# Key and value projections dealt anew around the third attention and the last attention's opening, and one key rotation moved behind two sums in the routed part

## The chip, the core and the metric

The kernel runs on one core of a Trainium2 chip. The core has five engines that each work through their own list of instructions and meet at semaphores: PE (TensorE: matrix products and transposes, written to eight PSUM banks), DVE (VectorE) and ACT (ScalarE), which both read PSUM, POOL (GpSimd), which works on SBUF, and SP (SyncE), which issues the DMAs here. The metric is the time of one execution on the device, in microseconds (us).

## What is computed

Eight layers work on x, 8 batches of 128 tokens of 512 numbers. Each takes the layer norm of x and adds its result to x:

```python
x = x + _L1_ffn_ref(_layernorm(x, axis=-1), ...)
x = x + _L2_xattn_ref(_layernorm(x, axis=-1), ctx_4096, L2_xattn_conv_w, L2_xattn_bn_gamma, L2_xattn_bn_beta)
x = x + _L2_ffn_ref(_layernorm(x, axis=-1), L2_ffn_W_base, L2_ffn_b_base, L2_ffn_W_router, L2_ffn_lora_A, L2_ffn_lora_B)
x = x + _L3_xattn_ref(_layernorm(x, axis=-1), ctx_4096, ctx_4096, mask_BxSxS2_ff0, L3_xattn_wq, L3_xattn_wk, L3_xattn_wv, L3_xattn_wo, 0)
x = x + _L3_ffn_ref(_layernorm(x, axis=-1), L3_ffn_route_w, L3_ffn_A, L3_ffn_Bw)
```

The change lies in three of them.

The third attention (`_L2_xattn_ref`) is not an attention by scores. It splits the channels into two sets, takes the maximum and the mean of each set for every token channel, runs a convolution of 7 taps over them, normalises the result over the whole batch, and scales the two sets with the sigmoids that come out.

The routed part (`_L2_ffn_ref`) is `x @ W_base.T + b_base` plus low-rank products of the two best of 8 experts.

The last attention (`_L3_xattn_ref`) has 32 query heads and 8 key and value heads of width 128. Queries and keys are turned by position: `x * cos + _rotate_half(x) * sin`. Its keys and values come from `ctx_4096`, an input, and not from x.

## The kernel before

**Work ahead.** Since the last attention's keys and values depend on the inputs alone, the kernel makes them earlier, in places where PE has time. The class `KeysAhead` (line 1632) deals them in 48 units: units 0 to 15 are halves of a key head (128 x 512 in PSUM), units 16 to 47 are values of one batch for two heads (128 x 256). One unit is 12 matmuls on PE: four chunks of the depth, each as hi x hi, hi x lo, lo x hi (lines 36 to 38). The units take turns in PSUM banks 6 and 7. Four methods hand the next units on, in the order in which the code calls them:

- `multiply(pe, count)`: PE makes the next `count` units. Unit u waits until unit u - 2 has been drained (`wait(pe, self.drained, u - 1)`, line 1698).
- `drain(act, count)`: ACT copies them from PSUM to `kv_keys` (line 1718) or `kv_values` (line 1721).
- `high(act, i)` and `low(pool, i)`: ACT and POOL split item i of the weights in two parts (lines 1685 and 1689). `high` of item i waits until all units of item i - 2 are made.
- `rotate(dve, count)` and `join(pool, count)`: DVE turns the next halves of the keys, each with two products into `kv_cross` (lines 1759 and 1760) and one into `kv_keys` (line 1764). POOL adds the two (line 1745).

**Third attention** (`l2_attention`, line 2121). It begins with `norm_stage` (line 109): DVE scales x to `l2x_xn` (line 136), PE turns it (line 171), ACT and DVE copy the turned batches out (lines 192 and 149). Its `pe_first` lets PE make three units ahead of the transposes. A block ends with a barrier of all engines. In the next block DVE masks four chunks (`l2x_fc`, line 2277), POOL takes the difference (`l2x_xn`, line 2182), DVE takes maxima and sums, and ACT takes the other means (line 2238, eight small instructions for each of six chunks). PE makes seven units meanwhile, and then turns the statistics (`l2x_stat`, line 2205). From there on it is a chain: the convolution on DVE (from line 2292), a product on PE, the mean and variance of the batch with two small products on PE (line 35, `l2x_zmv` and `l2x_dev`), the tanh on ACT (line 2253), transposes of the map on PE (line 2219), the scaling on ACT and DVE, transposes back (line 2227) and the sums to x (line 2344). PE makes three units beside the convolution, two behind the map and four behind the transposes back.

**Routed part** (`routed_ffn`, line 2349). PE makes 7 units and the first three base products, turns the weighted low-rank outputs (line 2445), and finishes batch after batch. Three PSUM banks serve the outputs: `base_product(b)` waits until DVE has added batch b - 3 to x (`wait(pe, o_read, b - 2)`, line 2430). DVE, which has its own list, rotates four halves of the keys before its first sum (line 2532), and one more before each of the sums 3 to 7.

**Last attention** (`l3_layer`, line 2658). `norm_stage` again, with three units ahead of the transposes and a split of the turned x in hi (ACT, line 184) and lo (DVE, line 141). In the next block PE projects the first query head in two halves, makes five units, and starts the scores of head 0 when POOL has joined both halves of the query. DVE rotates the two halves of the query (lines 1759, 1760, 1764 with `l3x_cross` and `l3x_q`), then two halves of the keys, and then masks the scores (line 3057). Eight groups of four heads follow; the first one still rotates three halves of the keys, and ACT copies the values (`l3x_v`, line 3015) when all sixteen are joined.

## Time and profile before

| | |
|---|---|
| Time, median of 3 runs | 1884.34 us (1883.32 to 1886.83) |
| Time of the profiled execution | 1882.91 us |
| Its span, first to last instruction | 1881.1 us |
| PE busy | 96% of the span |
| DVE, ACT, POOL busy | 72%, 34%, 33% |
| Mean granted clock of TensorE | 0.991 |
| DMA, mean | 42 GB/s |

The span is 1.8 us shorter than the time of its own execution. A row of the timeline gives the start and the length of one or more instructions in us from the span's start, then the engine, the line, what is written and read, and in brackets how long the engine sat idle before it, and what ended that. TensorE's granted clock is 1.00 at full speed (2.4 GHz) and 0.50 at half (1.2 GHz).

### The profile page before, as it was taken

What the parts mean: (1) busy time and instruction counts of PE and PEld (TensorE: products, weight loads), DVE (VectorE), ACT (ScalarE), POOL (GpSimd) and SP (SyncE); (2) the same over time, 40 slices, a digit from 0 to 9 for tenths busy, and PEclk for the clock granted to TensorE, in tenths of its full rate; (3) what the DMA queues carried; (4) which work ended last, traced back from release to release, by engine and by line L of the source; (5) the groups of instructions that cost most, each with busy time, mean ns of one, the idle gap of its engine ahead of it and who ended that gap; (6) DMA issues with size and microseconds to landing.
All of it is one profiled execution on the core that took longest, in us unless ns stands there. A gap on an engine that the chain in (4) does not pass through costs nothing. (4 is left out here: it accounts for less than half of the span.)

```text
span 1881.1 us, 29023 instructions
## 1 busy us (share of the span) xinstructions
PE 1802.9 (96%) x10418; PEld 1524.4 (81%) x10418; DVE 1348.7 (72%) x2778; ACT 636.4 (34%) x1749; POOL 615.0 (33%) x366
## 2 busy tenths in 40 slices
PE   7999999999999999998998998879899999999998
PEld 6888888899988888896876665665788888888886
DVE  5666676666666666657537877779788888888886
ACT  4312222222222221224025765530343343343333
POOL 6423322232223323323241003425433333334331
PEclk9999999999999999999999998989999999999999
DMA  4101111111001111110010002010101111110011
GB/s 172 59 7 50 50 52 49 52 49 52 25 23 52 49 52 49 52 54 23 23 45 20 1 26 68 23 63 1 45 24 45 34 33 33 34 33 33 34 34 46
DMA packets 29879, 78.44 MB, mean 42 GB/s; under 512 B 3856, under 2 KB 10704, under 8 KB 29424
## 3 DMA queue, kind: packets, MB, share of 16 engines
q1 hardware_dynamic: 29808, 77.50, 12.3%
q8 instruction: 44, 0.72, 0.2%
q14 instruction: 27, 0.22, 0.0%
HBM read 75.39 MB, written 2.10 MB: 41 GB/s over the span
## 5 line engine op out<-in xcount | busy, mean ns | idle before, releaser
L637 POOL TENSOR_TENSOR l0x_comb<-l0x_neg,l0x_bias 128x1024 f32<-128x1024 f32 x32 | 76.5, 2390 | 428.1 <-DVE l0x_probs L1002 305.2
L900 ACT ACTIVATE l0x_probs_t<-bank 128x512 f32<-128x512 f32 x32 | 19.1, 597 | 539.2 <-PE bank L753 539.2
L2795 POOL TENSOR_TENSOR l3x_q<-l3x_q,l3x_cross 128x512 f32<-128x512 f32 x64 | 89.7, 1406 | 194.4 <-DVE l3x_q L1764 194.4
L38 PE MATMUL bank<-l0x_w_v_hi,ctx_lo 128*128 128x256 f32 x512 | 144.9, 283 | 0.0
L37 PE MATMUL bank<-l0x_w_v_lo,ctx_hi 128*128 128x256 f32 x512 | 144.9, 283 | 0.0
L36 PE MATMUL bank<-l0x_w_v_hi,ctx_hi 128*128 128x256 f32 x512 | 144.9, 283 | 0.0
L886 ACT ACTIVATE l0x_probs<-l0x_probs,l0x_top 128x129 f32<-128x129 f32 x256 | 99.4, 390 | 61.1 <-DVE l0x_top L1006 61.1
L2981 ACT ACTIVATE l3x_probs<-l3x_probs,l3x_top 128x128 f32<-128x128 f32 x256 | 99.1, 388 | 38.1 <-DVE l3x_top L3062 38.0
L629 POOL TENSOR_TENSOR l0x_w_qk_lo<-l0x_raw_qk,l0x_w_qk_hi 128x1024 fp32r<-128x1024 f32 x31 | 75.0, 2420 | 110.5 <-ACT l0x_w_qk_hi L893 110.5
L36 PE MATMUL bank<-l3x_qin_hi,l3x_w_q_hi 128*128 128x512 f32 x256 | 105.8, 413 | 5.4 <-PEq L121 3.1
L36 PE MATMUL bank<-ctx_hi,l0x_w_qk_hi 128*128 128x512 f32 x256 | 100.8, 394 | 8.4 <-DVE ctx_lo L1113 8.4
L36 PE MATMUL bank<-l0x_qin_hi,l0x_w_qk_hi 128*128 128x512 f32 x256 | 105.4, 412 | 3.0 <-DVE l0x_qin_lo L1137 1.6
L1038 DVE TENSOR_TENSOR x<-x,bank 128x512 f32<-128x512 f32 x120 | 82.1, 684 | 33.2 <-PE bank L38 33.2
L37 PE MATMUL bank<-l3x_qin_lo,l3x_w_q_hi 128*128 128x512 f32 x256 | 100.7, 393 | 0.0
L38 PE MATMUL bank<-ctx_hi,l0x_w_qk_lo 128*128 128x512 f32 x256 | 100.6, 393 | 0.0
L37 PE MATMUL bank<-ctx_lo,l0x_w_qk_hi 128*128 128x512 f32 x256 | 100.5, 393 | 0.0
L38 PE MATMUL bank<-l3x_qin_hi,l3x_w_q_lo 128*128 128x512 f32 x256 | 100.5, 393 | 0.0
L38 PE MATMUL bank<-l0x_qin_hi,l0x_w_qk_lo 128*128 128x512 f32 x256 | 100.0, 391 | 0.0
L37 PE MATMUL bank<-l0x_qin_lo,l0x_w_qk_hi 128*128 128x512 f32 x256 | 99.9, 390 | 0.0
L37 PEld LDWEIGHTS bank<-l0x_w_v_lo,ctx_hi 128*128 128x128 f32 x512 | 98.2, 192 | 0.6
L36 PEld LDWEIGHTS bank<-l0x_w_v_hi,ctx_hi 128*128 128x128 f32 x512 | 98.2, 192 | 0.6
L38 PEld LDWEIGHTS bank<-l0x_w_v_hi,ctx_lo 128*128 128x128 f32 x512 | 98.2, 192 | 0.0
(474 smaller groups left out, 5222.2 us busy)
## 6 DMA issues: line engine op xcount, KB each, us to landing
l0x_raw_qk<-L_qk_dram SPq DMA_DIRECT2D x31, 512.0 KB, 4.7
l0x_raw_v<-L_v_dram SPq DMA_DIRECT2D x16, 512.0 KB, 5.6
l0x_raw_o<-L_o_dram SPq DMA_DIRECT2D x16, 512.0 KB, 5.3
l3x_raw<-L_q_dram SPq DMA_DIRECT2D x16, 512.0 KB, 3.4
l3x_raw<-L_o_dram SPq DMA_DIRECT2D x16, 512.0 KB, 3.4
kv_raw<-L_kv_dram SPq DMA_DIRECT2D x8, 512.0 KB, 3.5
l0x_ctx_raw<-ctx_t_dram SPq DMA_DIRECT2D x4, 512.0 KB, 5.9
x<-x_dram SPq DMA_DIRECT2D x8, 256.0 KB, 8.0
```

Of the source, the lines that this page charges most:

```text
L36: pe.matmul(out, lhs[0], rhs[0], start=start, stop=False)
L37: pe.matmul(out, lhs[0], rhs[1], start=False, stop=False)
L38: return pe.matmul(out, lhs[1], rhs[0], start=False, stop=stop)
L629: pool.tensor_tensor(f(w[1]), f(raw), as_f32(f(w[0])), ALU.subtract).then_inc(ready, 1)
L637: pool.tensor_tensor(comb[:, :, :], neg[:, :, :], bias[:, j:j + 1, :].to_broadcast([P, B, P]), ALU.add).then_inc(comb_ready, 1)
L886: act.activation(probs[j][:, b, :], probs[j][:, b, :], ACT.Exp, bias=top[:, b:b + 1], accum_out=row_sum[:, b:b + 1]).then_inc(exp_done, 1)
L900: act.activation(probs_t[:, 0:BH, :], bank[6][:, :].rearrange("p (b n) -> p b n", b=BH), ACT.Copy).then_inc(t_act, 1)
L1038: dve.tensor_tensor(x[:, b, :], x[:, b, :], bank[b % 4][:, :], ALU.add).then_inc(ring_drained, 1)
L2795: pool.tensor_tensor(dst[:, part], dst[:, part], cross[n][:, :], ALU.add).then_inc(rotated, 1)
L2981: act.activation(probs[j % 2][:, b, :], probs[j % 2][:, b, :], ACT.Exp, bias=top[:, b:b + 1], accum_out=row_sum[:, b:b + 1]).then_inc(exp_ ...
```

## The change

Nothing is computed that was not computed before, and no instruction is added or removed. Units, drains, rotations and joins change their places:

```diff
         def keys_before(act):
-            ahead.drain(act, 2)
+            ahead.drain(act, 1)
             ahead.high(act, 6)
             ahead.drain(act, 1)
 
-        norm_stage(core, xn, xt, loads, banks=6, pe_first=lambda pe: ahead.multiply(pe, 3), act_first=keys_before,
-                   pool_then=lambda pool: ahead.low(pool, 6))
+        norm_stage(core, xn, xt, loads, banks=6, pe_first=lambda pe: ahead.multiply(pe, 2), act_first=keys_before,
+                   pool_then=lambda pool: ahead.low(pool, 6), pe_then=lambda pe: ahead.multiply(pe, 1))
...
-                ahead.multiply(pe, 7)
+                ahead.multiply(pe, 6)
                 pe.wait_ge(stat_done, 1)
...
                 product(pe, bank[3][0:SETS * B, 0:1], [group], [dev[:, :]], True, True).then_inc(var_full, 1)
+                ahead.multiply(pe, 1)
                 pe.wait_ge(map_in, 1)
...
                         last.then_inc(means_done, 1)
-                        if (k, c) == (0, 1):
-                            ahead.drain(act, 2)
-                        if (k, c) == (0, 2):
-                            ahead.drain(act, 1)
+                        ahead.drain(act, 1)
+                        if (k, c) == (0, 3):
                             ahead.high(act, 7)
-                        if (k, c) == (1, 0):
-                            ahead.drain(act, 2)
                 ahead.drain(act, 2)
                 ahead.high(act, 8)
-                ahead.drain(act, 3)
+                ahead.drain(act, 2)
                 act.wait_ge(tanh_in, 1)
                 act.activation(z[:, :], z[:, :], ACT.Tanh, scale=0.5).then_inc(tanh_out, 1)
+                ahead.drain(act, 1)
                 act.wait_ge(map_done, 1)
...
                 if ahead:
-                    ahead.rotate(dve, 4)
+                    ahead.rotate(dve, 3)
                 if base:
                     dve.wait_ge(biased, B)
                 for b in range(B):
-                    if ahead and b >= 3:
+                    if ahead and b >= 2:
                         ahead.rotate(dve, 1)
...
             norm_stage(core, xn, qin, first_loads, first_high, first_low, banks=6,
-                       pe_first=lambda pe: ahead.multiply(pe, 3))
+                       pe_first=lambda pe: ahead.multiply(pe, 3), pe_then=lambda pe: ahead.multiply(pe, 2))
...
+                ahead.join(pool, 1)
                 rotate_both(0, q[0])
-                ahead.join(pool, 2)
+                ahead.join(pool, 1)
...
                 project_both(0, 0, w_q[0], 0, qin)
-                ahead.multiply(pe, 5)
+                ahead.multiply(pe, 3)
...
+                ahead.rotate(dve, 1)
                 for n in range(2):
                     rotate(n, 0, 0, 0, q[0], 0)
-                ahead.rotate(dve, 2)
+                ahead.rotate(dve, 1)
```

In the third attention the norm's PE work is now two units, the transposes, one unit (unit 4). The six units 5 to 10 stand ahead of the statistics' transposes, and unit 14 stands between the product of the variance and the transposes of the map. ACT drains one unit behind each of its six means. This is ACT's list behind the norm's copies, before and after; `l2x_stat` are the means, `kv_keys` the drains, `kv_w_hi` the weights' hi part. Before:

```order
L2238 ACTIVATE bank,l2x_stat<-l2x_fc 128x128 x16
L1718 ACTIVATE kv_keys<-bank 128x512 x2
L2238 ACTIVATE bank,l2x_stat<-l2x_fc 128x128 x8
L1718 ACTIVATE kv_keys<-bank 128x512
L1685 ACTIVATE kv_w_hi<-kv_raw 128x1024
L2238 ACTIVATE bank,l2x_stat<-l2x_fc 128x128 x8
L2238 ACTIVATE bank,l2x_stat<-l2x_xn 128x128 x8
L1718 ACTIVATE kv_keys<-bank 128x512 x2
```

And after:

```order
L2239 ACTIVATE bank,l2x_stat<-l2x_fc 128x128 x8
L1718 ACTIVATE kv_keys<-bank 128x512
L2239 ACTIVATE bank,l2x_stat<-l2x_fc 128x128 x8
L1718 ACTIVATE kv_keys<-bank 128x512
L2239 ACTIVATE bank,l2x_stat<-l2x_fc 128x128 x8
L1718 ACTIVATE kv_keys<-bank 128x512
L2239 ACTIVATE bank,l2x_stat<-l2x_fc 128x128 x8
L1718 ACTIVATE kv_keys<-bank 128x512
L1685 ACTIVATE kv_w_hi<-kv_raw 128x1024
L2239 ACTIVATE bank,l2x_stat<-l2x_xn 128x128 x8
L1718 ACTIVATE kv_keys<-bank 128x512
```

The first drain moved from behind the second mean to behind the first, and the weights' hi part from behind the third to behind the fourth.

In the routed part DVE's list changes around the first sums (`x<-x,bank` is a sum, the three lines ahead of it a rotation). Before, from the last of the four rotations on:

```order
L1759 TENSOR_TENSOR kv_cross<-kv_keys,kv_rope 64x512
L1760 TENSOR_TENSOR kv_cross<-kv_keys,kv_rope 64x512
L1764 TENSOR_TENSOR kv_keys<-kv_keys,kv_rope 128x512
L2532 TENSOR_TENSOR x<-x,bank 128x512
L88 BN_STATS stats<-x 128x6
L2532 TENSOR_TENSOR x<-x,bank 128x512
L88 BN_STATS stats<-x 128x6
L2532 TENSOR_TENSOR x<-x,bank 128x512
L88 BN_STATS stats<-x 128x6
```

And after, from the first sum on, which now follows the third rotation:

```order
L2530 TENSOR_TENSOR x<-x,bank 128x512
L88 BN_STATS stats<-x 128x6
L2530 TENSOR_TENSOR x<-x,bank 128x512
L88 BN_STATS stats<-x 128x6
L1759 TENSOR_TENSOR kv_cross<-kv_keys,kv_rope 64x512
L1760 TENSOR_TENSOR kv_cross<-kv_keys,kv_rope 64x512
L1764 TENSOR_TENSOR kv_keys<-kv_keys,kv_rope 128x512
L2530 TENSOR_TENSOR x<-x,bank 128x512
```

One rotation moved from ahead of the first sum to ahead of the third.

In the last attention two value units moved from behind the first query head to behind the norm's transposes, and DVE's list at the head of the block changes. Before:

```order
L1759 TENSOR_TENSOR l3x_cross<-bank,kv_rope 64x512
L1760 TENSOR_TENSOR l3x_cross<-bank,kv_rope 64x512
L1764 TENSOR_TENSOR l3x_q<-bank,kv_rope 128x512
L1759 TENSOR_TENSOR l3x_cross<-bank,kv_rope 64x512
L1760 TENSOR_TENSOR l3x_cross<-bank,kv_rope 64x512
L1764 TENSOR_TENSOR l3x_q<-bank,kv_rope 128x512
L1759 TENSOR_TENSOR kv_cross<-kv_keys,kv_rope 64x512
```

And after:

```order
L1759 TENSOR_TENSOR kv_cross<-kv_keys,kv_rope 64x512
L1760 TENSOR_TENSOR kv_cross<-kv_keys,kv_rope 64x512
L1764 TENSOR_TENSOR kv_keys<-kv_keys,kv_rope 128x512
L1759 TENSOR_TENSOR l3x_cross<-bank,kv_rope 64x512
L1760 TENSOR_TENSOR l3x_cross<-bank,kv_rope 64x512
L1764 TENSOR_TENSOR l3x_q<-bank,kv_rope 128x512
```

One rotation of the keys moved ahead of the two of the query; POOL's join of it moved in the same way.

## Rows read from the trace of the kernel before

**Rows 1.** Busy time and granted clock by stretch: us, PE, PEld, DVE, ACT, POOL, clock, DMA.

```profile
1224.00:1228.00 4.00, 0.56 (x5) 0.26 (x4) 2.27 (x8) 0.00 (x0) 0.33 (x1) 0.70 0.01 2
1228.00:1231.00 3.00, 0.04 (x1) 0.05 (x1) 1.90 (x4) 0.63 (x1) 0.20 (x1) 0.50 0.00 0
...
1338.00:1340.00 2.00, 1.92 (x5) 1.57 (x6) 0.00 (x0) 0.00 (x0) 0.00 (x0) 0.56 0.54 123
...
1390.00:1830.00 440.00, 439.72 (x2504) 382.91 (x2503) 374.60 (x513) 170.14 (x574) 152.08 (x86) 1.00 0.10 34
```

**Rows 2.** Timeline of DVE in the third attention.

```profile
1191.75 9.02 DVE L2277 TENSOR_TENSOR l2x_fc<-l2x_xt,crucial 128x1024 f32<-128x1024 f32 x4 [0.62 <-PEq L121]
...
1212.07 0.17 DVE L2286 TENSOR_SCALAR l2x_stat<-l2x_stat 128x16 f32<-128x16 f32 x1
1215.00 0.68 DVE L2292 COPY l2x_padded<-bank 32x512 f32<-32x512 f32 x1 [2.75 <-PE bank L2205]
```

**Rows 3.** Timeline of PE in the third attention.

```profile
1186.75 3.65 PE L171 MATMUL bank<-ident,l2x_xn 128*128 128x128 f32 x32
...
1208.71 0.47 PE L36 MATMUL bank<-kv_ctx_hi,kv_w_hi 128*128 128x512 f32 x1 [1.65 <-POOL kv_w_lo L1689]
...
1214.26 0.60 PE L2205 MATMUL bank<-ident,l2x_stat 128*32 128x128 f32 x4
...
1223.14 1.03 PE L35 MATMUL bank<-l2x_acc,l2x_pick 32*16 32x512 f32 x2
...
...
1230.95 0.61 PE L2219 MATMUL bank<-ident,l2x_z 16*128 16x16 f32 x4 [3.55 <-DVE l2x_z L2327]
1231.49 0.80 PE L36 MATMUL bank<-kv_ctx_hi,kv_w_hi 128*128 128x512 f32 x1
...
1236.35 0.28 PE L36 MATMUL bank<-kv_w_hi,kv_ctx_hi 128*128 128x256 f32 x1
```

**Rows 4.** Timeline of ACT in the third attention.

```profile
1207.99 1.05 ACT L1718 ACTIVATE kv_keys<-bank 128x512 f32<-128x512 f32 x2
```

**Rows 5.** Timeline of DVE in the routed part.

```profile
1294.81 0.69 DVE L1759 TENSOR_TENSOR kv_cross<-kv_keys,kv_rope 64x512 f32<-64x512 f32 x1
1295.50 1.66 DVE L1760 TENSOR_TENSOR kv_cross<-kv_keys,kv_rope 64x512 f32<-64x512 f32 x1
...
1297.81 0.68 DVE L2532 TENSOR_TENSOR x<-x,bank 128x512 f32<-128x512 f32 x1
...
1311.78 0.69 DVE L2532 TENSOR_TENSOR x<-x,bank 128x512 f32<-128x512 f32 x1 [0.73 <-PE bank L35]
```

**Rows 6.** Timeline of PE in the routed part.

```profile
1293.23 2.84 PE L35 MATMUL bank<-l2f_w_b,l2f_ht 128*128 128x512 f32 x6 [0.25 <-ACT l2f_ht L2471]
1298.63 1.10 PE L35 MATMUL bank<-l2f_w_base,l2f_xt 128*128 128x512 f32 x2 [2.56 <-DVE x L2532]
...
1303.00 3.60 PE L35 MATMUL bank<-l2f_w_base,l2f_xt 128*128 128x512 f32 x8
```

**Rows 7.** Timeline of PE at the last attention's opening.

```profile
1333.72 1.22 PE L171 MATMUL bank<-ident,l3x_xn 128*128 128x128 f32 x8 [1.05 <-DVE l3x_qin_lo L141]
1338.08 0.63 PE L36 MATMUL bank<-l3x_qin_hi,l3x_w_q_hi 128*128 128x512 f32 x1 [3.13 <-PEq L121]
...
1345.22 0.28 PE L36 MATMUL bank<-kv_w_hi,kv_ctx_hi 128*128 128x256 f32 x1
...
1352.41 1.95 PE L35 MATMUL bank<-kv_keys,l3x_q 128*128 128x128 f32 x16
...
1374.01 0.50 PE L36 MATMUL bank<-l3x_qin_hi,l3x_w_q_hi 128*128 128x512 f32 x1 [2.24 <-ACT l3x_v L3015]
```

**Rows 8.** Timeline of DVE at the last attention's opening.

```profile
1345.42 0.69 DVE L1759 TENSOR_TENSOR l3x_cross<-bank,kv_rope 64x512 f32<-64x512 f32 x1 [0.64 <-PE bank L38]
...
1347.55 0.69 DVE L1759 TENSOR_TENSOR kv_cross<-kv_keys,kv_rope 64x512 f32<-64x512 f32 x1
...
1353.74 1.36 DVE L3057 SCALAR_TENSOR_TENSOR l3x_probs<-bank,last_mask 128x512 f32<-128x512 f32 x2
```

## Prediction

> **What bounds the kernel now.** I read the windows first. Through the last attention's groups PE is busy for 439.72 of 440 us at full clock [rows 1]. So that stretch is PE's, and a head start or a delay that it gets at its opening comes out at the end of the kernel unchanged. Then I read PE's list for the places where it stands still between two layers, and asked for each who is late. There are four that the change touches.
>
> In the third attention the statistics' transposes start at 1214.26 [rows 3], though DVE finished the statistics at 1212.07 + 0.17 = 1212.24 [rows 2], and DVE then waits 2.75 us for them [rows 2]. Here PE is late: seven units stand ahead of the transposes. Behind the product of the variance it is PE that waits, 3.55 us [rows 3]. In the routed part PE waits 2.56 us for DVE's first sum [rows 6]. At the last attention's opening PE waits 3.13 us for the block's barrier, and then works at a granted clock of 0.56 [rows 7, 1].
>
> **Third attention, up to the statistics.** One 128 x 512 unit costs PE 2.78 us: two of them lie between 1208.71 and 1214.26, 5.55 us with the fill [rows 3]. Two units instead of three ahead of the norm's transposes let these begin at 1186.75 - 2.75 = 1184.0 [rows 3]. ACT has its drain and one weight split to do first, but copies the last batches in time, since it is paced by PE there. The transposes issue for 3.5 us, unit 4 follows for 2.75 us and the tail of its last matmul, so PE ends at about 1190.4. Before, the barrier followed 0.62 us behind DVE's last copy [rows 2]. The same 0.62 behind PE gives 1191.05 for DVE's start instead of 1191.75 [rows 2], so 0.7 us is gained and not 2.75, since PE is now the last at the barrier. If unit 4 hid nothing at all, the term would be 0; if the barrier needed nothing behind PE, 1.3.
>
> From its start to the finished statistics DVE needs 1212.24 - 1191.75 = 20.5 us [rows 2], so these are done at 1211.5. PE must have finished six units by then. Its bound is ACT: unit u waits for the drain of unit u - 2. The 1.65 us ahead of 1208.71 are laid to POOL's weight split by the view, but unit 10 needs unit 8 drained, and that is the first half of ACT's pair at 1207.99 [rows 3, 4]. Dealt one by one, ACT reaches the drain of unit 8 at about 1206.7 (0.7 earlier as the block is, and one drain less in its way), so unit 10 runs from 1207.3 to 1210.2. That is 1.3 us ahead of the statistics. If ACT were 1.3 us later than I count, the gain would shrink with it. The transposes start at about 1211.6 instead of 1214.26: **2.65 us**. Behind them PE has three units as before, and 1214.26 to 1223.14 [rows 3] is 8.9 us both for PE and for DVE's convolution; both shift alike.
>
> **Unit 14 in the gap.** It starts 0.1 us behind the variance product. PE stood idle for 3.55 us between that product and the transposes of the map [rows 3]. At full clock it takes 2.8 us and is hidden. But PE has done next to nothing since the convolution's product: the granted clock is 0.70 over 1224 to 1228, and 0.50 behind that [rows 1]. Its successor at half clock took from 1231.49 to 1236.35, 4.9 us and a tail of 0.15 [rows 3]; in the gap that is 1.5 to 1.6 us too long, and ACT, DVE and POOL all wait for the map. The bounds are 0 and 1.6. The stretch of the 0.70 row is the very place, so I take the middle, **0.8 us lost**. What it frees behind the map is worth nothing: there PE makes two units either way, while ACT scales.
>
> The Trainium skill ("TensorE: Matmul & The Clock Gate", Part 1) says that the array falls to 1.2 GHz when idle, and that the counting runs free, so that the point varies from run to run. The rows show the fall, not yet the spread. By this rule unit 14 would cost something between nothing and 1.6 us, another amount in each run, and the sum below would scatter by as much.
>
> **Routed part.** The fourth rotation starts at 1294.81 and the first sum at 1297.81 [rows 5]: it is 3.0 us long, as one of its products took 1.66 us and not 0.69 [rows 5], with POOL's join beside it. With three rotations the first sum starts at 1294.8 and is done at 1295.5. Its product is ready: three outputs are made from 1293.23 to 1296.07 [rows 6], one each 0.95. So base product 3 is free at 1295.5 and PE takes it when it is through with the third output, at 1295.9, instead of 1298.63 [rows 6]: **2.7 us**. From there on PE is the slower of the two; DVE waited 0.73 us for each of the later sums [rows 5]. The moved rotation costs DVE 2.1 to 3.1 us ahead of the third sum, which then comes at 1299.5 to 1300.5. Base product 5 needs it. A batch of PE's is 1303.00 - 1298.63 = 4.4 us long [rows 6], so that is two batches behind 1295.9, at 1304.6. That is 4 us of cover. If it were gone, every us more would come off the 2.7. POOL's join of that rotation moves with it and is waited for by nobody before the next rotation but one. The stage ends with PE's three units and their drain, so the whole 2.7 goes on.
>
> **Last attention's opening.** From PE's start to the scores pass 1352.41 - 1338.08 = 14.33 us [rows 7]. Of these, the five units are 7.19 us [rows 7], 1.44 each; two of them go to the norm, 2.88 us. The projection of the first head, 24 matmuls, takes 1345.22 - 1338.08 = 7.14 us [rows 7], where the same number took 5.55 at full clock [rows 3]. PE had stood still for 3.13 us. With two units in that gap, from 1334.8 to 1337.8, it should not fall, and 1.6 us come back. Against that stand 0.2 us, since PE's tail is now as late at the barrier as DVE. Sum: **4.3 us**; if the clock falls all the same, 2.7.
>
> DVE must follow. Before, it rotated the second half of the query from 1345.42 to 1347.55, two halves of keys from there to 1353.74, 3.1 each, and took the scores at 1353.74, 1.33 behind their start [rows 8, 7]. Now one rotation fits ahead of the query: it starts with the block, takes 2.1 us, and the query's first half comes out of PE 2.9 us in. The second half is out at 1343.9, rotated at 1346.0, the one key behind it at 1349.1. PE's scores start at 1348.1, and DVE wants them at 1349.4. POOL's join of the second query half, 1.8 us at most, ends at 1347.9, so PE, DVE and POOL meet within 0.3 us. Moving only the units or only the rotation would give little. Behind the scores nothing changes: three rotations stay in the first group, and PE's wait of 2.24 us for the values' copy [rows 7] stays with them.
>
> **The sum.** 2.65 - 0.8 + 2.7 + 4.3 = 8.85 us. Against the profiled execution that is 1882.91 - 8.9 = 1874.0. The median of the runs was 1884.34, 1.4 us above that execution, so I forecast 1884.34 - 8.9 = **1875.4 us**.
>
> **The rivals.**
>
> *The clock takes part of it.* Unit 14 runs wholly at 1.2 GHz (0.8 us more) and the opening's projection too (1.6 us). For: both stand next to idle stretches, and rows 1 show half clock at both places. Against: at the opening the idle time is filled. 8.9 - 2.4 = 6.5 us gained, 1877.8 us. Chance 0.17.
>
> *The head start of the last attention is given back.* The first group waits for the joined keys and for ACT's copy of the values. If that chain, or the DMA of the mask that is issued with the block, did not move with the scores, the 4.3 us would end in a longer wait than 2.24 there. Against: the chain is counted from the scores on, in the same order. 4.6 us gained, 1879.7 us. Chance 0.10. With the clock's losses too, 1882.1 us, no difference to speak of: 0.05.
>
> *Slower: a long stretch at half clock.* In the last attention PE has no idle time, so every us at 1.2 GHz there costs 0.5 us. The new timing would have to drop the clock after PE's 2.24 us wait and hold it for long: from 17.8 us of half clock on the 8.9 are eaten, from 25.4 us on the kernel is more than 0.2% slower, with 1888.2 us or more. The row of 440 us at 1.00 [rows 1] speaks against it. Chance 0.03.
>
> **How the numbers follow.** The forecast has 0.65; its own range is 1872.8 to 1877, from unit 14 free and 0.6 more at the barrier, and a median lower by the 1.4 us that lie between profile and median here, up to unit 14 at 1.6 and an opening 0.8 short. Adding the first rival and the nearer part of the second gives 1872.8 to 1879.2. A measurement of this kernel tells 0.2%, 3.8 us, from no change: below 1880.6 lie the forecast and the first two rivals, 0.92; 0.05 lies within; 0.03 above.
>
> **What would show it.** In the profile after: the statistics' transposes within 0.3 us of DVE's last statistic, and DVE's 2.75 us wait below 1; unit 14 either 2.8 us long, or up to 5 us with matmuls of 0.8 us and a map that waits for it; no wait of PE for DVE's sum in the routed part; no half clock at the last attention's opening, and 10 us from PE's start there to the scores. The prediction is wrong if PE, and not DVE, is again the last at the statistics, or if PE's wait for the values' copy grows from 2.24 to 5 us or more.

## The result, and the profile after

| | before | after |
|---|---|---|
| Time, median of 6 runs each | 1884.2 us (1883.32 to 1887.37) | 1876.67 us (1875.39 to 1878.11) |
| Time of the profiled execution | 1882.91 us | 1875.39 us |
| Its span | 1881.1 us | 1873.6 us |
| Mean granted clock | 0.991 | 0.991 |

The ratio of the times is 0.995, with a 95% interval of 0.9938 to 0.9961. The interval lies below 1, so the kernel is faster, by 7.5 us or 0.4%. PE is busy for nearly the same time, 1805.0 us after and 1802.9 before, 96% of the span in both.

I compare stages by the time that has passed since the third attention's norm began (DVE's first L131 there; at 1178.35 before, 1177.88 after). What lies ahead of that point is untouched, and the point moved by up to 5 us between the profiles of this study, so its own place says nothing about the change.

| us from the norm's start | before | after | earlier |
|---|---|---|---|
| DVE's statistics done | 33.89 | 33.17 | 0.72 |
| their transposes on PE | 35.91 | 33.24 | 2.67 |
| transposes of the map on PE | 52.60 | 50.95 | 1.65 |
| transposes back on PE | 64.39 | 62.55 | 1.84 |
| next norm begins | 76.48 | 75.26 | 1.22 |
| last attention's norm begins | 147.01 | 142.98 | 4.03 |
| scores of head 0 on PE | 174.06 | 165.78 | 8.28 |
| first `l3x_heads_lo` on DVE | 203.84 | 196.88 | 6.96 |
| end | 702.75 | 695.72 | 7.03 |

The last row and the 0.47 us of the starting point make the 7.5; the 0.47 are no work of the change. PE's timeline in the third attention, after; start, length and work in us, and in brackets the idle time ahead and what ended it:

```profile
1211.12 0.61 PE L2205 MATMUL bank<-ident,l2x_stat 128*32 128x128 f32 x4 [0.96 <-DVE l2x_stat L2284]
...
1224.16 0.20 PE L35 MATMUL bank<-l2x_dev,l2x_mean 16*16 16x1 f32 x2 [1.07 <-DVE l2x_dev L2315]
1224.29 0.50 PE L36 MATMUL bank<-kv_ctx_hi,kv_w_hi 128*128 128x512 f32 x1
...
1228.83 0.42 PE L2220 MATMUL bank<-ident,l2x_z 16*128 16x16 f32 x4
...
1240.43 6.24 PE L2228 MATMUL bank<-ident,l2x_fc 128*128 128x128 f32 x32 [6.81 <-DVE l2x_fc L2338]
```

PE now waits for the statistics and not they for PE (against the row at 1214.26 in [rows 3]). Unit 14 fills the gap, but it takes all from 1224.29 to 1228.83, and the map's transposes wait for nothing but it. The transposes back, 6.24 us here, come behind 6.81 us of idle. DVE's timeline there:

```profile
1190.57 9.01 DVE L2275 TENSOR_TENSOR l2x_fc<-l2x_xt,crucial 128x1024 f32<-128x1024 f32 x4 [2.62 <-PEq L121]
...
1210.88 0.17 DVE L2284 TENSOR_SCALAR l2x_stat<-l2x_stat 128x16 f32<-128x16 f32 x1
1211.87 0.68 DVE L2290 COPY l2x_padded<-bank 32x512 f32<-32x512 f32 x1 [0.81 <-PE bank L2205]
...
1253.14 0.64 DVE L131 BATCH_NORM_AGGREGATE mv<-stats 128x2 f32<-128x6 f32 x8 [0.93 <-PEq L2166]
```

DVE waits 0.81 us for the statistics' transposes where it waited 2.75 [rows 2], but 0.93 us at the barrier that ends the layer. The granted clock by stretch (us, PE, PEld, DVE, ACT, POOL, clock, DMA): unit 14, the transposes back, and the first group of the last attention behind PE's wait for the values' copy:

```profile
1224.00:1226.00 2.00, 1.83 (x8) 1.49 (x9) 1.03 (x4) 0.00 (x0) 0.53 (x1) 0.79 0.01 4
1226.00:1228.00 2.00, 2.00 (x7) 1.52 (x6) 1.13 (x3) 0.63 (x1) 0.00 (x0) 0.50 0.00 0
...
1240.00:1246.00 6.00, 5.57 (x28) 5.57 (x29) 4.69 (x8) 0.71 (x2) 2.35 (x1) 0.53 0.00 0
...
1334.00:1344.00 10.00, 10.00 (x63) 9.01 (x63) 8.39 (x11) 1.35 (x5) 4.37 (x3) 1.00 0.33 107
...
1365.00:1367.00 2.00, 2.00 (x5) 1.62 (x6) 1.97 (x3) 1.91 (x5) 1.05 (x1) 0.53 0.00 0
1367.00:1369.00 2.00, 2.00 (x7) 1.52 (x7) 1.94 (x4) 2.00 (x11) 1.33 (x1) 0.62 0.00 0
```

The row of 1334 to 1344 is the last attention's opening, all of it at full clock, where 0.56 was granted over two of these microseconds [rows 1]. The last two rows are new. This is the same place in the kernel before, right behind the same wait, at a clock of 1.00:

```profile
1374.00:1376.00 2.00, 1.99 (x9) 1.65 (x10) 1.97 (x3) 1.91 (x5) 1.02 (x1) 1.00 0.00 0
```

The timeline of PE shows the routed part and the opening, after:

```profile
1292.49 1.88 PE L35 MATMUL bank<-l2f_w_b,l2f_ht 128*128 128x512 f32 x4
1294.21 3.60 PE L35 MATMUL bank<-l2f_w_base,l2f_xt 128*128 128x512 f32 x8
...
1333.79 0.47 PE L36 MATMUL bank<-l3x_qin_hi,l3x_w_q_hi 128*128 128x512 f32 x1 [0.32 <-PEq L121]
1343.66 0.80 PE L35 MATMUL bank<-kv_keys,l3x_q 128*128 128x128 f32 x5
...
1364.98 0.69 PE L36 MATMUL bank<-l3x_qin_hi,l3x_w_q_hi 128*128 128x512 f32 x1 [1.89 <-ACT l3x_v L3014]
```

The fourth base product, the first of the row at 1294.21, follows without a wait (2.56 us in [rows 6]). The barrier costs PE 0.32 us instead of 3.13 and the scores start 9.87 us behind the projection instead of 14.33 [rows 7]. The wait for the values' copy is 1.89 us (2.24 before).

**Where the time went.** Ahead of the scores 8.28 us are gained. The first group gives 1.3 back. The loss lies between the start of ACT's copy of the values and the first `l3x_heads_lo`, a stretch of 10.9 us that was 9.3 before.

### The profile page after: what moved, and what is told of

It is laid out like the page before. It is cut to its first block and busy times, and to the rows that moved or that the text cites. A ratio compares the mean times of both kernels' runs of the same rounds, so it can differ in the third digit from the quotient of the medians.

```text
span 1873.6 us, 29023 instructions
## 1 busy us (share of the span) xinstructions
PE 1805.0 (96%) x10418; PEld 1525.9 (81%) x10418; DVE 1345.4 (72%) x2778; ACT 635.6 (34%) x1749; POOL 614.0 (33%) x366
```

## The experiments: each part alone

The three parts of the change were put one by one into the kernel before. The diffs are against it.

**The third attention's part alone**

```diff
-            ahead.drain(act, 2)
+            ahead.drain(act, 1)
...
-        norm_stage(core, xn, xt, loads, banks=6, pe_first=lambda pe: ahead.multiply(pe, 3), act_first=keys_before,
-                   pool_then=lambda pool: ahead.low(pool, 6))
+        norm_stage(core, xn, xt, loads, banks=6, pe_first=lambda pe: ahead.multiply(pe, 2), act_first=keys_before,
+                   pool_then=lambda pool: ahead.low(pool, 6), pe_then=lambda pe: ahead.multiply(pe, 1))
...
-                ahead.multiply(pe, 7)
+                ahead.multiply(pe, 6)
...
+                ahead.multiply(pe, 1)
                 pe.wait_ge(map_in, 1)
```

(ACT's drains as in the change.)

> The kernel before with the third attention's part of the change alone. Theory (each part gains by itself): the statistics' transposes come about 2.65 us earlier, unit 14 in the gap gives back 0.8 to 1.0 us of it, and the end of the layer gives back another 0 to 0.6 us, since the transposes back run at half clock. 1.2 to 1.9 us gained, about 1882.6 us beside a median of 1884.2. Rival (it is worth nothing by itself, all the gain is elsewhere): 1884.2 us.

Measured: 1885.66 us against 1885.25 of the kernel before in the same set of runs, ratio 0.9995 (0.9984 to 1.0005). No gain is seen, as the rival had it, but the interval still holds the 1.2 us of the theory, so the times decide nothing. The profile (of the slowest of its 12 executions, 1888.63 us) tells more. The statistics' transposes stand at 33.28 us and the next norm at 75.30, as after. But the last attention's norm begins at 147.45, later than the 147.01 before. DVE at the end of the layer has the same longer wait as after:

```profile
1257.54 0.65 DVE L131 BATCH_NORM_AGGREGATE mv<-stats 128x2 f32<-128x6 f32 x8 [0.93 <-PEq L2166]
```

So this part gains 1.2 us at its own end, and in this profile nothing of it reached the last attention. PE still waits 2.56 us for DVE's first sum in the routed part, as in [rows 6], and here the clock falls behind that wait:

```profile
1302.00:1304.00 2.00, 2.00 (x3) 0.67 (x2) 1.93 (x4) 0.00 (x0) 0.00 (x0) 0.50 0.00 0
```

DVE's first sum is still 1.2 us earlier than before, the next norm 0.4 us later. The same wait of 2.56 us had no fall behind it in the kernel before, and in the whole change the wait is gone. The first group of the last attention had a fall too, and the end came 1.8 us later (704.56).

**The routed part alone**

```diff
-                    ahead.rotate(dve, 4)
+                    ahead.rotate(dve, 3)
...
-                    if ahead and b >= 3:
+                    if ahead and b >= 2:
```

> The kernel before with three rotations ahead of the sums and the fourth ahead of the third sum, and nothing else. Theory: PE's wait of 2.56 us for DVE's first sum is gone, base product 3 follows the third output at once, and the layer ends 2.7 to 2.8 us earlier: 1881.5 us. Rival (DVE becomes the bound further on, because the moved rotation delays the third sum): PE waits again for the third to sixth sum, less than 1.5 us gained, 1883 us or more.

Measured: 1882.54 us, 0.9986 (0.9977 to 0.9995). The last attention's norm begins at 144.20 instead of 147.01, 2.81 us earlier. The end is only 1.48 us earlier (701.27): here too the first group has a fall behind PE's wait for the values' copy. The wait is 2.25 us, and its row comes first:

```profile
1371.64 0.50 PE L36 MATMUL bank<-l3x_qin_hi,l3x_w_q_hi 128*128 128x512 f32 x1 [2.25 <-ACT l3x_v L3015]
```

```profile
1371.00:1373.00 2.00, 1.36 (x6) 1.15 (x7) 1.97 (x4) 2.00 (x3) 0.39 (x1) 1.00 0.00 0
1373.00:1377.00 4.00, 4.00 (x16) 3.35 (x15) 3.76 (x7) 3.21 (x17) 3.12 (x2) 0.57 0.21 40
```

**The last attention's opening alone**

```diff
-                       pe_first=lambda pe: ahead.multiply(pe, 3))
+                       pe_first=lambda pe: ahead.multiply(pe, 3), pe_then=lambda pe: ahead.multiply(pe, 2))
...
+                ahead.join(pool, 1)
                 rotate_both(0, q[0])
-                ahead.join(pool, 2)
+                ahead.join(pool, 1)
...
-                ahead.multiply(pe, 5)
+                ahead.multiply(pe, 3)
...
+                ahead.rotate(dve, 1)
                 for n in range(2):
                     rotate(n, 0, 0, 0, q[0], 0)
-                ahead.rotate(dve, 2)
+                ahead.rotate(dve, 1)
```

> The kernel before with the last attention's opening changed and nothing else (two units behind the norm's transposes, one key rotation ahead of the query's). Theory: the scores of head 0 start 4.2 to 4.3 us earlier and keep it, unless the granted clock falls behind PE's wait for the values' copy, which would take 1.3 to 1.7 us back in that run: 1879.9 us, or 1881.4 in runs with the fall. Rival (the head start is given back in the first group for good, through the chain of joined keys): PE's wait for the values' copy grows and 1882.5 us or more come out in all runs.

Measured: 1880.72 us, 0.9973 (0.996 to 0.9986). The scores start at 169.67, 4.39 us earlier, and the end is 4.74 us earlier. PE's wait for the values' copy is 1.89 us, to the hundredth as after, yet the clock behind it stays up. First the timeline of PE, then the windows:

```profile
1369.67 0.50 PE L36 MATMUL bank<-l3x_qin_hi,l3x_w_q_hi 128*128 128x512 f32 x1 [1.89 <-ACT l3x_v L3016]
```

```profile
1370.00:1372.00 2.00, 2.00 (x10) 1.66 (x9) 1.97 (x3) 1.92 (x7) 1.35 (x1) 1.00 0.00 0
```

A matmul of 0.50 us is one at full clock, the 0.69 after is not. From the scores to the first `l3x_heads_lo` this kernel takes 29.5 us and the changed one 31.1, and 1.6 us is about what 3.4 us at half clock cost.

**The whole change once more**, beside the three.

> The changed kernel once more, unchanged, for a second profile of it. In its first profile the granted clock was half for 3.4 us in the last attention's first group, right behind PE's wait of 1.89 us for the values' copy; in the kernel before a wait of 2.24 us at the same place left it at full. Theory (that fall comes in some executions and not in others): this profile may be without it, and is then 1.3 to 1.7 us shorter from the second head on; the same for the half clock in unit 14, which may last from 2.8 to 5 us. Rival (it belongs to the new timing): the fall stands at the same place again.

Measured: 1875.68 us, 0.9946 (0.9931 to 0.996), against the same runs of the kernel before (1885.25) as the three parts. The ratios of the parts, 0.9995, 0.9986 and 0.9973, would make 0.9954 together, inside that interval, so the times don't show whether the parts help each other. The profiles do: from the norm to the end the parts are 1.8 us later, 1.5 earlier and 4.7 earlier, 4.4 us together, and the whole is 7.0 earlier. The parts have three falls of the clock that the kernel before has not, two in the first group and one in the routed part, and the whole has one. At about 1.6 us each, an estimate from the first group, this is enough for the difference.

By its median this set has the change 9.6 us faster, the first set 7.5. The landmarks agree with those of the first profile of the changed kernel within 0.2 us (end at 695.5), and the fall in the first group stands in the same place of the program:

```profile
1366.00:1368.00 2.00, 1.55 (x4) 1.27 (x5) 1.97 (x4) 1.91 (x4) 0.57 (x1) 0.68 0.00 0
1368.00:1370.00 2.00, 2.00 (x6) 1.52 (x6) 1.94 (x4) 2.00 (x11) 1.80 (x1) 0.50 0.00 0
```

## The experiments: halves of the opening, and fewer rotations

**Only the two units** behind the norm's transposes, and **only the rotation and join** ahead of the query (against the kernel before):

```diff
-                       pe_first=lambda pe: ahead.multiply(pe, 3))
+                       pe_first=lambda pe: ahead.multiply(pe, 3), pe_then=lambda pe: ahead.multiply(pe, 2))
...
-                ahead.multiply(pe, 5)
+                ahead.multiply(pe, 3)
```

> The kernel before with two units behind the last attention's norm transposes, and nothing else: both key rotations stay behind the query's. Theory (PE and DVE are tied at the opening): no half clock, the scores start 4.2 us earlier, but DVE masks them only 1.6 us earlier, since two key rotations of 3.1 us each stand ahead; 1.6 us gained. Rival (PE alone is the bound): the mask comes 4.2 us earlier too.

```diff
+                ahead.join(pool, 1)
                 rotate_both(0, q[0])
-                ahead.join(pool, 2)
+                ahead.join(pool, 1)
...
+                ahead.rotate(dve, 1)
                 for n in range(2):
                     rotate(n, 0, 0, 0, q[0], 0)
-                ahead.rotate(dve, 2)
+                ahead.rotate(dve, 1)
```

> The kernel before with one key rotation and its join ahead of the query's at the last attention's opening, and nothing else. Theory (PE and DVE are tied): DVE is free for the scores at 12.6 us from PE's start in the block, but the scores start at 14.3 us as before and the mask follows 1.3 us behind; less than 0.2 us gained there. Rival (DVE alone is the bound): the mask comes 3 us earlier.

Measured, against 1884.72 of the kernel before: units 1884.55 us, 0.9998 (0.9987 to 1.0009); rotation 1884.49 us, 0.9994 (0.9984 to 1.0004). The timeline of the units' kernel has PE's first scores at 1350.06 and DVE's first mask 4.19 us later (1.33 before, [rows 7, 8]):

```profile
1350.06 1.13 PE L35 MATMUL bank<-kv_keys,l3x_q 128*128 128x128 f32 x8
```

```profile
1354.25 1.28 DVE L3057 SCALAR_TENSOR_TENSOR l3x_probs<-bank,last_mask 128x512 f32<-128x512 f32 x2
```

PE is 4.5 us early, DVE 1.6 us. Of these 1.6 only 0.2 are left at the end, since PE's wait for the values' copy grows to 2.94 us and the clock falls there:

```profile
1374.00:1378.00 4.00, 3.53 (x9) 2.81 (x10) 3.91 (x7) 3.91 (x14) 2.38 (x1) 0.57 0.00 0
```

With the rotation alone it is DVE that waits for the scores:

```profile
1356.34 0.69 DVE L3058 SCALAR_TENSOR_TENSOR l3x_probs<-bank,last_mask 128x512 f32<-128x512 f32 x1 [2.90 <-PE bank L35]
```

The mask is 0.2 us early, as the theory had it. But the key that was rotated sooner also brings the values' copy sooner, PE waits 1.21 us for it and not 2.24, and the end is 1.0 us earlier:

```profile
1375.74 0.50 PE L36 MATMUL bank<-l3x_qin_hi,l3x_w_q_hi 128*128 128x512 f32 x1 [1.21 <-ACT l3x_v L3016]
```

So the profiles show 0.2 us for the units, 1.0 for the rotation and 4.7 for both; the times tell neither half from no change. The claim "Moving only the units or only the rotation would give little" holds, though the units' 0.2 owe something to the clock.

**Two rotations ahead of the sums** instead of four, and one more ahead of each from the second on (against the kernel before, so beside the routed part alone):

```diff
-                    ahead.rotate(dve, 4)
+                    ahead.rotate(dve, 2)
...
-                    if ahead and b >= 3:
+                    if ahead and b >= 1:
```

> The kernel before with only two rotations ahead of the routed part's sums, and one ahead of each sum from the second on. Theory (with three rotations PE is already bound by its own third output): base product 3 starts behind the third output at 2.7 us earlier than before, no more than with three. Rival (DVE's first sum is still the bound with three): one rotation less gives up to 0.5 us more.

Measured: 1882.81 us, 0.9986 (0.9977 to 0.9996); the last attention's norm at 144.21, where three rotations gave 144.20. DVE's first sum now waits for PE:

```profile
1295.95 0.69 DVE L2532 TENSOR_TENSOR x<-x,bank 128x512 f32<-128x512 f32 x1 [2.81 <-PE bank L35]
```

So the change took all that was to be had here; a second rotation moved leaves DVE idle and PE as it was. The clock differs behind that point all the same: at the last attention's opening it is at half for 6.8 us and not 3.4, and behind the first group's wait of 2.26 us it does not fall. The end is that of three rotations.

## The experiments: the clock

From here on the edits are made to the changed kernel. The question is whether the terms that came out short were lost to the clock, and whether they can be had back.

**The wait for the values behind more work.** PE waits for ACT's copy of the values in the first group ahead of the second half of a projection. Here the wait stands behind that half and the last two units:

```diff
-                    if j == 1:
+                    if j == 1 and not units:
                         pe.wait_ge(v_ready, g + 1)
...
                         ahead.multiply(pe, units, 2)
+                        pe.wait_ge(v_ready, g + 1)
```

> The changed kernel; in the last attention's first group PE waits for the values' copy only behind the second half of the next query head and the last two units, and not ahead of them. Theory (PE's idle 1.89 us makes the clock fall there, and the fall is what the head start lost): PE works through, no half clock behind it, and the second head's work is 1.3 to 2 us earlier than in the changed kernel's profiles: 1874.5 us. Rival (DVE and POOL, which join the last keys, are the bound there and not PE): PE's wait only moves behind the units, and the end comes at most 0.5 us earlier: 1876 us.

Measured: 1874.34 us, 0.9936 (0.9921 to 0.9951). The first `l3x_heads_lo` comes at 194.09 instead of 196.88, and the end at 693.01 instead of 695.72. The windows over the place of the old wait and over the stretch that fell after. Counted from the norm, which starts at 1181.39 in this profile, that stretch begins at 1368.6:

```profile
1364.00:1370.00 6.00, 6.00 (x32) 5.09 (x31) 4.53 (x6) 2.64 (x4) 2.52 (x3) 1.00 0.00 0
1368.00:1373.00 5.00, 4.07 (x30) 3.67 (x28) 4.88 (x7) 4.91 (x20) 2.79 (x2) 1.00 0.09 9
```

PE has no idle time up to the end of the two units, and the clock stays at 1.00. Behind them it stands still for 1.61 us, where it was 0.47, so a part of the wait has only moved:

```profile
1373.68 2.02 PE L35 MATMUL bank<-l3x_probs_t,l3x_v 128*128 128x128 f32 x16 [1.61 <-issue]
```

The 2.8 us up to `l3x_heads_lo` are the 1.6 that the change lost there and 1.2 more. The interval overlaps that of the change, so the profile shows the gain and the times alone don't.

**The gap of unit 14 filled.** 14 transposes of the identity into a bank that nobody reads, ahead of the mean's product, and 7 ahead of the variance's. They compute nothing that is used.

```diff
+                for _ in range(14):
+                    pe.transpose(bank[5][:, 0:P], core.ident[:, :], core.ident[:, :])
                 pe.wait_ge(mean_in, 1)
...
+                for _ in range(7):
+                    pe.transpose(bank[5][:, 0:P], core.ident[:, :], core.ident[:, :])
                 pe.wait_ge(var_in, 1)
```

> The changed kernel with 14 and 7 extra transposes of the identity, to a PSUM bank that nobody reads then, in PE's two waits ahead of unit 14 (1.78 and 1.07 us before). Theory (unit 14 is long because the clock fell for want of work): unit 14 takes 2.8 us and not 4.6, and the transposes of the map start 0.8 to 0.9 us earlier from the norm on. Rival (the unit is long for another cause, such as its weights or its bank): it stays at 4.6 us.

Measured: 1876.9 us, 0.9946 (0.9929 to 0.9963), in 3 runs. PE's timeline, and the windows over unit 14:

```profile
1228.96 0.20 PE L35 MATMUL bank<-l2x_dev,l2x_mean 16*16 16x1 f32 x2 [0.16 <-DVE l2x_dev L2319]
...
1232.71 0.42 PE L2224 MATMUL bank<-ident,l2x_z 16*128 16x16 f32 x4 [0.60 <-DVE l2x_z L2329]
```

```profile
1229.00:1233.00 4.00, 3.40 (x18) 2.54 (x18) 2.04 (x5) 1.17 (x2) 0.53 (x1) 1.00 0.01 2
```

Unit 14 runs at full clock, PE again waits for the map (0.60 us), and the map's transposes stand at 49.98, 2.62 us earlier than before: the whole 2.65 of the first term. The next norm begins at 73.68, 1.58 us earlier than after. The first group's fall is gone too, though nothing was done there (wait 1.91 us), and the end is at 692.37, 3.35 us earlier than after. The median doesn't show that: this profile's third attention begins at 1182.73, 4.9 us later than after's. So the stage is shown, the gain of the whole kernel isn't.

**The idle time ahead of the transposes back filled**, with 52 such transposes behind the two units:

```diff
                 ahead.multiply(pe, 2)
+                for _ in range(52):
+                    pe.transpose(bank[5][:, 0:P], core.ident[:, :], core.ident[:, :])
```

> The changed kernel with 52 extra transposes of the identity, to a PSUM bank that nobody reads then, in PE's wait of 6.8 us ahead of the transposes back. Theory (the third attention ended 1.2 us and not 1.8 earlier, because the transposes back ran at half clock for 6.8 us and the units behind them became the last): no half clock there, the transposes back take 3.6 to 5.3 us and not 6.2, DVE is again the last, and the next norm starts 0.6 us earlier or a little more. Rival (the end of the layer is bound by the barrier itself): no change in the next norm's start.

Measured: 1878.41 us, 0.9957 (0.994 to 0.9973). PE's timeline:

```profile
1244.38 3.71 PE L2230 MATMUL bank<-ident,l2x_fc 128*128 128x128 f32 x32 [1.14 <-DVE l2x_fc L2340]
```

The transposes back take 3.71 us instead of 6.24, and the next norm begins 1.07 us earlier (74.19). But now the clock falls in the routed part's opening, where it had not:

```profile
1258.00:1262.00 4.00, 4.00 (x28) 4.00 (x28) 3.36 (x8) 0.77 (x2) 0.61 (x1) 0.77 0.94 320
```

The fall begins 0.4 us behind the norm's start, and PE's row there shows a longer wait than the 0.88 us after:

```profile
1256.17 0.36 PE L36 MATMUL bank<-kv_w_hi,kv_ctx_hi 128*128 128x256 f32 x1 [2.32 <-PEq L2166]
```

PE was done earlier with the transposes back and the units, so it waited longer for the layer's end. From that norm to DVE's first `l2f_h` the kernel takes 31.32 us instead of 29.87. That is 1.45 more, so what was won is lost again in the next part. The first group had no fall in this profile, which is why the end is 1.25 us earlier than after (694.47); the median isn't.

**The late wait with the filled gap**, and **with both places filled**:

```diff
+                for _ in range(14):
+                    pe.transpose(bank[5][:, 0:P], core.ident[:, :], core.ident[:, :])
                 pe.wait_ge(mean_in, 1)
...
+                for _ in range(7):
+                    pe.transpose(bank[5][:, 0:P], core.ident[:, :], core.ident[:, :])
                 pe.wait_ge(var_in, 1)
...
                         ahead.multiply(pe, units, 2)
+                        pe.wait_ge(v_ready, g + 1)
```

> The changed kernel with both: PE waits for the values' copy behind the last two units, and 14 and 7 extra transposes of the identity to a bank that nobody reads then fill PE's waits ahead of unit 14. Theory (the two repair different places): the third attention ends 1.6 us earlier, as with the extra transposes alone, and the first group's second head is 2.8 us earlier than that, or 1.2 if the clock would not have fallen there anyway; 1872.3 to 1873.5 us. Rival (both take away the same 2.7 us, the fall in the last attention): about 1874.3 us, as with the late wait alone.

Measured: 1874.3 us, 0.9941 (0.9929 to 0.9952), which is the rival's number and not the theory's. The second kernel has the 52 transposes as well:

```diff
                 ahead.multiply(pe, 2)
+                for _ in range(52):
+                    pe.transpose(bank[5][:, 0:P], core.ident[:, :], core.ident[:, :])
```

> The changed kernel with the late wait for the values' copy, the 14 and 7 extra transposes ahead of unit 14 and the 52 extra transposes ahead of the transposes back (all of the identity, to a bank that nobody reads then). Theory (each half clock that is taken away gives its own time): on top of the late wait alone, 0.9 to 1.0 us in the gap of unit 14 and 1.0 to 1.1 at the layer's end; 1872.3 us. Rival (the fall only moves: with 52 transposes ahead of the transposes back one appeared in the routed part's opening): one of the two terms is given back behind the layer, 1873.5 to 1874.5 us.

Measured: 1873.4 us, 0.9942 (0.9928 to 0.9956). Here too the rival is the nearer one (1873.5 to 1874.5 against 1872.3). It is the lowest median of the study, but no interval parts these two from the late wait alone or from the change itself. In the second kernel the next norm begins at 73.18, and the fall stands again in the routed part's opening:

```profile
1254.00:1259.00 5.00, 5.00 (x35) 5.00 (x35) 4.17 (x9) 1.37 (x3) 0.06 (x1) 0.75 0.72 273
```

The first kernel is the same program as the filled gap alone up to the last attention. Its map stands at 49.97 too (49.98), but its next norm begins at 74.71, 1.03 us later than there. Row by row: the transposes back of the filled gap, and then those of this kernel:

```profile
1244.31 5.07 PE L2232 MATMUL bank<-ident,l2x_fc 128*128 128x128 f32 x32 [6.80 <-DVE l2x_fc L2342]
```

```profile
1240.34 6.66 PE L2232 MATMUL bank<-ident,l2x_fc 128*128 128x128 f32 x32 [6.81 <-DVE l2x_fc L2342]
```

The same work behind the same idle time, and 1.6 us apart: the clock came back later in one profile than in the other.

## Why the prediction was right, and where its terms were off

It forecast 1875.4 us with 1872.8 to 1879.2; measured were 1876.67 us, 7.5 us less than before where 8.9 were forecast. The second set of runs has 1875.68 and 9.6 us less. The profiles, which leave out what lies ahead of the norm, have 7.0 and 7.2 us.

**Third attention up to the statistics, 2.65: measured 2.67.** DVE starts 0.7 us earlier as said (1190.57 and not 1191.75, of which 0.47 is the starting point of the profile), 0.61 us behind PE's unit 4. ACT paced unit 10 in time: PE waits 0.96 us for the statistics.

**Unit 14 in the gap, -0.8: measured -1.0.** Of the 2.67, 1.65 are left at the map. The unit took 4.5 us, where the bounds of 0 and 1.6 lost went by 2.8 and 4.9. The filled gap shows the cause: with the clock up it cost nothing. The bounds held, and the row of 0.70 was rightly read as the place.

**"What it frees behind the map is worth nothing": it cost 0.4.** This is the first mis-sized term. I had set it at zero because PE makes two units there either way. But they now run at full clock and are done early. That gains 0.2 us up to the transposes back and loses 0.6 behind them (1.65, 1.84 and 1.22 in the table): PE stands idle for 6.81 us ahead of them (4.79 before), and they took 6.24 us instead of 5.32. PE came last at the layer's barrier, and DVE waited 0.93 us there instead of 0.32. The filled stretch, with its 3.71 us and a wait of 0.32 again, shows that the clock is behind this.

**Routed part, 2.7: measured 2.81**, and 2.81 with this part alone. PE's wait of 2.56 us is gone, and the moved rotation was covered: even a second one moved left the end of the part where it was.

**The opening, 4.3: measured 4.25**, at a clock of 1.00, the scores 9.87 us behind PE's start where "10 us" was named. Both halves of it are needed, which the two kernels with one half show.

**"Behind the scores nothing changes": it cost 1.25.** This is the second mis-sized term, and the larger. PE's wait for the values' copy did not grow, it shrank by 0.35 us. But the clock fell behind it, which it had not done before, and PE's restart came 1.6 us further ahead of the first `l3x_heads_lo`. I had this in view only as the slower rival, priced from 17.8 us of half clock on. It came with 3.4 us, too short to make the kernel slower and long enough to cost more than any error of the other terms. The late wait and the opening alone, where the clock did not fall behind the same 1.89 us, show it.

Summed from norm to end: 1.22 in the third attention, 2.81, 4.25, less the 1.25 of the first group make 7.03, and the 0.47 of the starting point make 7.5. The forecast had 8.85. So the mechanism was right, and two terms set at nothing were off, by 1.7 us together; the other terms erred by 0.2 us at most. That the profile comes to 7.5 and not 7.0 is luck of the starting point. Of the rivals the first, that the clock takes part, was at work beside the forecast: in part at unit 14, where it was placed, not at the opening, where it was placed too, and at two places where the sum had zero.

Two numbers of the forecast don't add up, without weight for the outcome. With the head start given back, the opening's 1.6 us can't be lost once more, so that rival with the clock's losses is 1880.5 us and not 1882.1. And the lower end of the range, from its own terms, is 1872.6 and not 1872.8.

**The spread of the clock.** By the rule of the Trainium skill ("TensorE: Matmul & The Clock Gate", Part 1) that the counting runs free, unit 14's cost should have differed between runs. The two profiles of the changed kernel don't show that: the unit took 4.5 us in both, and the third attention's transposes back 6.24 and 6.23. In all eleven profiles in which the gap was not filled, the half clock there begins 47.2 to 47.4 us behind the norm's start. What does agree with the rule are the two kernels of 5.07 and 6.66 us, alike up to that point, and the stretch ahead of the norm, in which all kernels are alike. Here PE restarts there behind the same wait of 2.03 us, with the row and the window of the filled gap first and those of the kernel before behind them:

```profile
863.47 0.47 PE L841 MATMUL bank<-l0x_w_o_hi,l0x_heads_hi 128*128 128x512 f32 x1 [2.03 <-issue]
```

```profile
864.00:869.00 5.00, 5.00 (x16) 3.98 (x15) 0.73 (x1) 0.00 (x0) 0.00 (x0) 0.66 0.00 0
```

```profile
862.15 0.47 PE L841 MATMUL bank<-l0x_w_o_hi,l0x_heads_hi 128*128 128x512 f32 x1 [2.03 <-issue]
```

```profile
863.00:868.00 5.00, 4.75 (x27) 3.87 (x26) 1.01 (x2) 0.60 (x1) 0.00 (x0) 1.00 0.00 0
```

The clock fell behind it in one profile and not in the other, and 1.6 us were lost: the first profile was 1.3 us behind the second at this row, and 2.9 us some 6 us later. Ahead of the norm the half clock adds up to 17.1 us in five profiles, which reach the norm at 1178.3 to 1178.9, and to 23.9 us in five, which reach it at 1181.1 to 1182.7; the other four have 20.5 us and 1177.9 to 1180.5. So the moving starting point goes with falls of the clock in code that nobody touched. How much of the scatter of the times comes from this is open.

**What stays open.** Why the clock falls behind the wait of 1.89 us in the changed kernel and not behind the same wait in the kernel with the opening alone. The fall also stood there with the third attention's part alone and with the routed part alone (wait 2.25 us in both) and with the two units alone (2.94 us). It was absent in the kernel before (2.24 us), with two rotations (2.26 us), with the rotation at the opening alone (1.21 us) and in the two with one filled place of the third attention (1.91 and 1.89 us). The length of the wait doesn't tell these apart. Nor does the fall follow the wait at a fixed distance: it begins 0.1 us behind its end in the changed kernel and 1.4 us behind it with the routed part alone. It may be the place in time that decides, but no run was made that shifts the same wait by parts of a microsecond.

## What to carry to other kernels

Where an engine waits at the joint of two layers, move work into the wait from behind it, but ask on every engine who would then be last: PE's units without DVE's rotation, or the rotation without the units, gave 0.2 and 1.0 us of the 4.7. Count what a faster stretch leaves idle. PE's idle time that is moved, not removed, can take the clock down at a place that was never touched, and a term set at zero for "it only shifts" deserves a bound of 1 to 2 us. A wait that stands in the middle of PE's work goes behind the work that doesn't need it; in the profile that edit of one line's place gave 2.7 us more (693.01 for 695.72), though its ratio, 0.9936, is not one that the intervals part from the change itself.

## What the runs showed of the hardware

- Behind the same wait of PE, the granted clock fell to half for 3.4 us in some kernels (wait 1.89, 2.25 and 2.94 us) and stayed at 1.00 in others (1.89, 1.91, 2.24 and 2.26 us). The changed kernel, profiled twice, had the fall twice.
- Filling one idle stretch of PE with 52 transposes took the half clock from there and set a fall elsewhere: 1.07 us gained at the layer's end, 1.45 us lost in the next part, behind an idle time of 2.32 us that had been 0.88.
- 14 and 7 transposes in the waits ahead of unit 14 kept the granted clock at 1.00; with only the two small products there it was 0.79 and then 0.50.
- Behind 6.8 us of idle the same 32 transposes took 5.07, 6.24 or 6.66 us, by when the clock came back, and 3.71 us where PE had been kept busy.
- In code that all kernels share, behind the same wait of 2.03 us, the clock fell in one profile and stayed at 1.00 in another, for 1.6 us. All of the half clock in that shared code came to 17.1 us in five profiles and to 23.9 us in five others.
